# A scan and expert-routing kernel: GpSimd makes every third drive product, a third state buffer, earlier weight loads and separate gates

## The chip, the cores and the metric

The kernel runs on one core of a Trainium2 chip. The metric is the device time of one execution in microseconds (us).

The engines, as the profile names them, are PE (TensorE, matrix products; PEld its weight loads), DVE (VectorE), ACT (ScalarE), POOL (GpSimd) and SP (SyncE, which here only issues DMAs). Each works through its own queue of instructions in order and waits on semaphores for the others. SBUF is the on-chip memory, PSUM the memory in which PE accumulates.

## The reference

Four images of 64x64x3 become 256 tokens each (three levels of patches in Hilbert order, fused by one linear layer) and 128 text tokens are put behind them: 4 sequences of L = 384 tokens with C = 192 features, 1536 tokens in all. Then

```
h = concat(tokenizer(x), txt)
h = h + block(layernorm(h))        # a selective state-space block
h = h + moe(layernorm(h))          # 8 experts, top 2 per token

block:  x, z = split(x @ in_proj.T);  u = silu(causal_conv(x))
        dt = softplus(u @ dt_w.T + dt_b);  B = u @ B_w.T;  C = u @ C_w.T
        state[t] = exp(dt*A) * state[t-1] + dt*B*u        # for 16 states s
        y = sum over s of state*C, + D*u;  y = (y*silu(z)) @ out_w.T
        return layernorm(y + residual) * g + b
moe:    top 2 of h @ Wr.T, gates = softmax of the two
        out = sum of gate_k * (gelu(h @ Wi_e.T + bi_e) @ Wo_e.T + bo_e)
```

## The kernel before, in words

**Stages.** The tokenizer gathers patches with indirect DMAs, PE makes the levels and the fused tokens. Each of three chunks of 128 tokens (of all four sequences at once) is normed, projected, convolved and turned into dt, B and C. B and C rows are written to DRAM (`bc_dram`) and read back broadcast over the partitions. Then come the 48 steps of the scan, the routing, and a loop over 31 tiles of 128 slots each, every tile of one expert.

**A step.** Step `at` is chunk n = at // 16 and state s = at % 16. The instructions of one step lie on all engines:

- PE spreads row B into PSUM, `wide(at % 2)`, and adds up, two steps late, the products of state and C (`sum_states(at - 2)`, L1005 and L1007); between these it has filler and pieces of other stages.
- DVE makes the drive product dt*u*B in place in `wide` (L1752) and then scans (L1760): state = decay * state + drive along the tokens, into `states[at % 2]`. It needs that the product of step at-2 has read that buffer (`hc_rdy`).
- ACT makes the decay (L1437, L1438), saves the last state of each chunk (L1443) and carries it into the next chunk (L1455).
- POOL makes the state product hc = state * C (L697). C rows lie in a ring of RING = 3 buffers, hc in two.
- SP issues the C row three steps ahead (`broadcast_c`, L561 and L563: three DMAs), once the product of step at-3 is made.

In 8 of the 48 steps (at % 6 == 5, `by_pool`) POOL makes the drive as well (L686), from a B row that SP has broadcast to SBUF (`broadcast_b`), into `decay[2]`; DVE then only scans, and ACT puts the decay into PSUM.

**What is put between the steps.** For chunks 1 and 2, DVE handles the chunk before: its output (s = 1), residual (7), scores and the new rows of h (8), the top two (9), a shift (10). ACT writes the router rows (s = 12) into the tile of rows `xf`, SP sends them to `x_dram` (L590) at s = 14 of chunks 1 and 2. SP also issues 20 pieces of expert weights (289 KB each, L583), from step 16 on at steps with at % 4 != 3, and three whole experts after the last sum.

**Routing.** DVE makes from the top two of each token a slot number (counting by PE, prefix sums), then the gates (L1953 to L1956), one-hot tables (L1959 to L1969), which PE turns into a token number for each slot (L1129). POOL fetches the rows of the first four tiles (L706) from `x_dram`, whose rows hold x and, in the last columns, the two gates, sent by L593. It goes once `x_sent` counts all of these. PE meanwhile adds the experts' biases (L1143, L1149) and runs filler. Each tile is transposed (L1161), goes through up (L1171, L1179), gelu on ACT and down (L1190), is scaled by its gate on ACT and added into `sum_dram` by POOL (L722). At the end four DMAs copy it to the output (L639).

Filler are matmuls without use (`keep_warm`, L934), whose number at each place stands in the table `WARM`.

## Time and profile before

| | us |
|---|---|
| runs | 427.67, 433.89, 433.04 |
| median | 433.04 |
| the profiled execution | 433.38 |
| its span | 431.6 |
| granted TensorE clock, mean over the span | 0.941 |

The busy time over the whole span:

| engine | busy us | share |
|---|---|---|
| PE | 379.8 | 88% |
| DVE | 276.2 | 64% |
| POOL | 224.0 | 52% |
| ACT | 200.5 | 46% |

The span is what the trace covers, 1.8 us less than the run's own time. The shares are averages over stages that differ much, and a part of PE's time is filler, so the table alone doesn't tell what sets the time. The stages can be told apart by the lines: steps are L1752, L1760, L697 and L1005, from about 77 to 241 us of the span, and the loop over tiles is L1171 to L1190, from 276 us on.

### The profile page before, as it was taken

How to read it: one execution, taken by the hardware profiler on the slowest of the kernel's cores; microseconds unless marked ns; L12 is line 12 of the kernel's file. 1: busy time of each engine (PE TensorE's matmuls, PEld its weight loads, DVE VectorE, ACT ScalarE, POOL GpSimd, SP SyncE). 2: the span in 40 equal slices, each digit the busy share in tenths (PEclk: the TensorE clock that was granted, in tenths of full speed). 3: DMA queues.
4: the chain of work that ended last, by engine and by line, in shares of the span. 5: the costliest groups of instructions: out<-in, count | busy, mean ns of one | idle time of the engine just before them, and what ended most of it. 6: DMA issues, size and time to landing. Idle time of an engine off the chain costs nothing.

```text
span 431.6 us, 6906 instructions
## 1 busy us (share of the span) xinstructions
PE 379.8 (88%) x2285; PEld 286.8 (66%) x2285; DVE 276.2 (64%) x511; ACT 200.5 (46%) x516; POOL 224.0 (52%) x166
## 2 busy tenths in 40 slices
PE   5799989979996995779968898999999999999970
PEld 4465756646564662445634486799999999999970
DVE  4605456999899998997999596643444534434400
ACT  1347447674853546734547023144444354354440
POOL 6877730564636772756637200345565554655531
PEclk9969899999989996998979997799999999999995
DMA  6401103446574875497857544433333233232224
GB/s 168 78 6 11 7 3 70 122 120 137 116 147 122 232 243 165 158 270 210 294 167 189 150 209 74 113 83 59 49 46 61 43 49 56 44 52 48 39 28 118
DMA packets 37351, 46.98 MB, mean 109 GB/s; under 512 B 9485, under 2 KB 25950, under 8 KB 36750
## 3 DMA queue, kind: packets, MB, share of 16 engines
q1 hardware_dynamic: 29998, 38.94, 32.1%
q0 software_dynamic: 7328, 7.74, 12.2%
q8 instruction: 12, 0.20, 0.2%
q14 instruction: 13, 0.11, 0.1%
HBM read 40.65 MB, written 7.19 MB: 111 GB/s over the span
## 4 chain that ended last, share of the span: by engine, by line
PE 60%; DVE 17%; ACT 6%; DMA 5%; POOL 5%; issue 3%; SPq 1%; POOLq 0%; DVEq 0%; ACTq 0%
PE ps L1190 15%; PE ps L1171 10%; PE ps L1179 6%; DVE w_all L1760 5%; PE ps L1005 4%; DMA w_all<-bc_dram 3%; PE ps L1053 3%; PE ps L934 3%; POOL w_all L647 3%; POOL w_all L697 2%; DVE ps L1752 2%; PE ps L1007 2%; PE ps L1161 2%; DVE stats L1586 1%; DVE h_tok L1807 1%
## 5 line engine op out<-in xcount | busy, mean ns | idle before, releaser
L697 POOL TENSOR_TENSOR w_all<-w_all 128x768 f32<-128x768 f32 x47 | 78.9, 1682 | 82.4 <-DVE w_all L1760 36.6
L722 POOL DMA_INDIRECT sum_dram<-u_cm,tok_row x31 | 50.9, 1641 | 60.5 <-ACT u_cm L1551 53.8
L1005 PE MATMUL ps<-w_all,cst 128*128 128x512 f32 x96 | 55.4, 661 | 22.9 <-POOL w_all L697 22.3
L1760 DVE TENSOR_TENSOR_SCAN w_all<-decay,ps 128x780 f32<-128x780 f32 x40 | 71.1, 1779 | 2.0 <-POOL w_all L697 0.7
L706 POOL DMA_INDIRECT dt_cm<-x_dram,tok_in x31 | 30.8, 993 | 41.0 <-DVE texi L1989 29.0
L647 POOL DMA_INDIRECT w_all<-in_pix,gidx x42 | 44.1, 1051 | 14.9 <-issue 12.5
L1536 ACT ACTIVATE u_cm<-ps,x_cm 128x128 f32<-128x128 f32 x96 | 26.5, 376 | 39.8 <-PE ps L1179 39.8
L934 PE MATMUL ps<-cst 128*128 128x256 f32 x132 | 36.5, 433 | 5.5 <-DMA cst<-in_cst 4.9
L1005 PEld LDWEIGHTS ps<-w_all,cst 128*128 128x128 f32 x96 | 16.5, 198 | 35.4 <-POOL w_all L697 30.4
L1752 DVE TENSOR_TENSOR ps<-dtu_cm,ps 128x768 f32<-128x768 f32 x40 | 38.0, 949 | 2.7 <-ACT ps L1455 2.5
L1536 ACT ACTIVATE z_cm<-ps,y_cm 128x128 f32<-128x128 f32 x90 | 24.8, 375 | 27.5 <-PE ps L1179 27.5
L934 PEld LDWEIGHTS ps<-cst 128*128 128x128 f32 x132 | 28.0, 219 | 12.6 <-DMA cst<-in_cst 4.9
L2001 DVE COPY x_cm<-w_all 128x1154 f32 x16 | 12.2, 762 | 37.1 <-PE ps L1190 37.1
L1007 PEld LDWEIGHTS ps<-w_all,cst 128*128 128x128 f32 x96 | 19.2, 200 | 24.9 <-issue 24.9
L1190 PE MATMUL ps<-x_cm,u_cm 128*128 128x192 f32 x192 | 35.5, 333 | 0.0
L1053 PE MATMUL ps<-cst 128*128 128x256 f32 x122 | 33.6, 401 | 0.0
L1190 PE MATMUL ps<-y_cm,z_cm 128*128 128x192 f32 x180 | 33.4, 334 | 0.0
L2001 DVE COPY y_cm<-w_all 128x1154 f32 x15 | 11.4, 762 | 33.0 <-PE ps L1190 33.0
L1437 ACT ACTIVATE decay<-dt_cm,a_neg 128x512 f32<-128x512 f32 x40 | 28.4, 711 | 8.2 <-DVE dt_cm L1709 8.1
L1190 PEld LDWEIGHTS ps<-x_cm,u_cm 128*128 128x128 f32 x192 | 31.0, 189 | 1.8
L1190 PEld LDWEIGHTS ps<-y_cm,z_cm 128*128 128x128 f32 x180 | 29.0, 189 | 1.8
L1007 PE MATMUL ps<-w_all,cst 128*128 128x256 f32 x96 | 30.1, 396 | 0.0
(268 smaller groups left out, 706.8 us busy)
## 6 DMA issues: line engine op xcount, KB each, us to landing
w_all<-bc_dram SPq DMA_DIRECT2D x48, 256.0 KB, 3.6
w_all<-bc_dram SPq DMA_DIRECT2D x96, 64.0 KB, 3.8
w_all<-in_w_all SPq DMA_DIRECT2D x20, 289.0 KB, 4.5
w_all<-in_w_all SPq DMA_DIRECT2D x3, 1156.0 KB, 8.9
b_wide_sb<-bc_dram SPq DMA_DIRECT2D x8, 256.0 KB, 3.9
x_dram<-x_cm SPq DMA_DIRECT2D x3, 384.0 KB, 4.6
sum_dram<-h_tok SPq DMA_DIRECT2D x3, 384.0 KB, 4.3
out<-sum_dram SPq DMA_DIRECT2D x4, 288.0 KB, 3.7
```

What stands on the lines that cost most here:

```text
L647: pool.indirect_dma_start(dst, None, d[table], bass.IndirectOffsetOnAxis(ap=gidx[:, col:col + 1].bitcast(U32), axis=0)).then_inc(signal, 16)
L697: nc.gpsimd.tensor_tensor(segments(hcs[at % 2]), inner(states[at % 2]), segments(c_sb[at % RING]), ALU.mult).then_inc(hc_rdy, 1)
L722: pool.indirect_dma_start(sum_dram, bass.IndirectOffsetOnAxis(ap=tok_row[:, i:i + 1].bitcast(U32), axis=0), y_out[:, i % 2, :], None, comp ...
L934: nc.tensor.matmul(ps[:, bank, 0:256], ident, cst[:, 0:256], start=True, stop=True)
L1005: nc.tensor.matmul(sums[:, 0:4 * P], ident, hcs[at % 2][:, 0:4 * P], start=False, stop=at % S == S - 1, skip_group_check=True)
L1007: nc.tensor.matmul(sums[:, 4 * P:6 * P], ident, hcs[at % 2][:, 4 * P:6 * P], start=False, stop=at % S == S - 1, skip_group_check=True).the ...
L1053: nc.tensor.matmul(ps[:, bank, 256:512], ident, cst[:, 0:256], start=False, stop=True, skip_group_check=True)
L1171: nc.tensor.matmul(ps[:, 2 + 2 * p + f // 3, P * (f % 3):P * (f % 3) + P], w[:, W_UA + P * f:W_UA + P * f + P], xe[:, p, 0:P], start=(f % ...
L1190: mm = nc.tensor.matmul(ps[:, 6 + p, 0:C], hid[p][:, P * f:P * f + P], w_now[p][:, W_DN + C * f:W_DN + C * f + C], start=(f == 0), stop=(f ...
L1536: ins = nc.scalar.activation(hid[p][:, P * f:P * f + P], ps[:, 2 + 2 * p + f // 3, P * (f % 3):P * (f % 3) + P], ACT.Gelu, bias=w_now[p][: ...
L1752: v.tensor_tensor(inner(wide(p)), chunk(dtu3, n), inner(wide(p)), ALU.mult).then_inc(driven, 1)
L1760: v.tensor_tensor_scan(states[p], fade, drive, 0.0, ALU.mult, ALU.add).then_inc(scanned, 1)
```

## The change

- **Drives on POOL.** `by_pool` is true for every third step from 5 on (5, 8, ..., 47): 15 instead of 8 drives. B rows for them are issued three steps ahead into the one buffer `b_wide_sb`.
- **Third state buffer.** The scan of step `at` writes `states[at % 3]` and needs the product of step at-3 instead of at-2.
- **Weight pieces.** 7 of the 20 pieces are issued right behind the first stored B and C rows, 5 more at the odd steps 7 to 15, the last 8 at every third step from 16 on. For this the tokenizer's temporary tiles, which lie in the weights' memory, are put in another order.
- **Rows and gates apart.** Rows go both to `x_first` and to `x_dram` (two DMAs each), for chunk 0 at step 34 and for chunk 1 after the loop. Gates get a tile and a table of their own (`gate_x`, `gate_dram`). The first four fetches read `x_first` and need only the rows; four fetches of gates follow.
- **Order between the steps.** DVE makes the top two in front of the new h, and the shift a step later; ACT's deviation and router rows move a step later too.
- **Start.** PE's products with the router weights move behind the coarse rows, the first rows of the residual behind the fused tokens; filler is set anew.
- **Routing.** Tables are laid out [k, expert, token], so that operations read in order; the gates' arithmetic moves behind the one-hot tables; the low one-hots are made in four parts; the last product, sum and output of the scan go in halves; the last bias rows move from ahead of the first tile to behind its up projection.
- **Output.** Two of the four final DMAs are issued by ACT.

The core of the diff:

```diff
-        states = [scan_buffer(WIDE) for _ in range(2)]
+        states = [scan_buffer(WIDE) for _ in range(2)] + [third_state[:, :]]
...
-        WARM = {"input weights": 10, "coarse levels": 2, "fine patches": 2, "patches": 7, "normed rows": 7, "convolution": 2,
-                "first step": 10, "last rows": 11, "slots": 20, "bias rows": 1, "first tile": 4}
+        WARM = {"input weights": 10, "coarse levels": 2, "fine patches": 2, "patches": 7, "normed rows": 4, "convolution": 2,
+                "first step": 10, "last rows": 11, "slots": 18, "bias rows": 1, "first tile": 3}
...
-            return at % 6 == 5
+            return at > RING and at % RING == RING - 1
 
         def pool_drives(at):
-            return (at + 1) // 6
+            return max(0, (at + 1) // RING - 1)
 
...
-                if at >= 6:
-                    sp.wait_ge(pool_driven, pool_drives(at - 6))
+                if at >= 2 * RING:
+                    sp.wait_ge(pool_driven, pool_drives(at - RING))
...
+            def rows_of(dst, j, columns):
+                return dst.rearrange("(b j p) c -> j p b c", b=NB, j=NJ)[j, :, :, columns]
 
             def send_rows(j):
                 sp.wait_ge(xf_rdy, j + 1)
-                sp.dma_start(x_rows(j, 0, C), xf[:, NB * j:NB * j + NB, 0:C]).then_inc(x_sent, 16)
+                for dst, signal in ((x_first, x_sent), (x_dram, rows_sent)):
+                    sp.dma_start(rows_of(dst, j, slice(0, C)), xf[:, NB * j:NB * j + NB, 0:C]).then_inc(signal, 16)
+                    sp.dma_start(rows_of(dst, j, slice(C, CW)), xf[:, NB * j:NB * j + NB, P:C]).then_inc(signal, 16)
 
             def send_gates(j):
-                sp.dma_start(x_rows(j, C, XW), xf[:, NB * j:NB * j + NB, P:XF]).then_inc(x_sent, 16)
+                for dst, columns in ((gate_dram, slice(0, TOPK)), (x_dram, slice(CW, XW))):
+                    sp.dma_start(rows_of(dst, j, columns), gate_x[:, NB * j:NB * j + NB, :]).then_inc(gates_sent, 16)
 
             loads = [(e, p) for e in (*range(E - LATE), E - 1) for p in range(PIECES)]
 
             store_bc(0)
+            sp.wait_ge(coarse_ps, 4)
+            sp.wait_ge(rearr, 2)
+            for piece in loads[0:7]:
+                load_expert(*piece, PIECES)
+            loaded = 7
             store_bc(1)
...
-            router_weights()
+            keep_warm(WARM["coarse levels"], 4)
             coarse_levels()
+            pe.wait_ge(ld_mix, 16 * N_MIX)
             pe.wait_ge(x_out, 2)
             dt_low(0)
             dt_high_and_bc(0)
             coarse_rows()
             keep_warm(WARM["fine patches"], 0)
-            first_rows()
...
-                if by_pool(at - RING) and at - RING + 6 < STEPS:
-                    broadcast_b(at - RING + 6)
-                if at > S and at % S == 14:
-                    send_rows(at // S - 1)
+                if by_pool(at) and at + RING < STEPS:
+                    broadcast_b(at + RING)
+                if at == 2 * S + 2:
+                    send_rows(0)
+                if at == 7:
+                    sp.wait_ge(fused_ps, 2)
                 if at == S:
                     sp.wait_ge(xt_ready, 6)
                     sp.wait_ge(dtu_rdy, 3)
+                    sp.wait_ge(mixed_ps, 1)
                 if at == 2 * S + 7:
                     sp.wait_ge(summed, 2 * S + 1)
                     sp.dma_start(u_cm[:, 0:N_TAB // 2], d["cst"][:, N_CST:N_CST + N_TAB // 2]).then_inc(ld_tab, 16)
-                if at >= S and at % 4 != 3 and loaded < len(loads):
+                if (7 <= at < S and at % 2 == 1 or at >= S and at % 3 == 1) and loaded < len(loads):
                     load_expert(*loads[loaded], PIECES)
                     loaded += 1
             assert loaded == len(loads)
...
-                if by_pool(at + RING):
+                if by_pool(at + RING) and at + RING < STEPS:
...
+            def fetch(i, src, columns, signal):
+                pool.indirect_dma_start(x_in[:, i % NX, columns], None, src, bass.IndirectOffsetOnAxis(
+                    ap=tok_in[:, i:i + 1].bitcast(U32), axis=0)).then_inc(signal, 16)
...
+                fetch(i, x_first, slice(0, CW), xin_l[i])
+            pool.wait_ge(gates_sent, 16 * 2 * NJ)
+            for i in range(NX):
+                fetch(i, gate_dram, slice(CW, XW), gate_l[i])
+            pool.wait_ge(rows_sent, 16 * 2 * NJ)
...
+            def last_sum():
+
+                pe.wait_ge(last_hc, 1)
+                nc.tensor.matmul(sums[:, 0:4 * P], ident, hcs[(STEPS - 1) % 2][:, 0:4 * P], start=False, stop=True,
+                                 skip_group_check=True).then_inc(last_low, 1)
+                pe.wait_ge(last_hc, 2)
+                nc.tensor.matmul(sums[:, 4 * P:6 * P], ident, hcs[(STEPS - 1) % 2][:, 4 * P:6 * P], start=False, stop=True,
+                                 skip_group_check=True).then_inc(summed, 1)
 
...
-                if at >= 2:
-                    dve.wait_ge(hc_rdy, at - 1)
-                    if at - 2 < STEPS - S:
-                        dve.wait_ge(carry_saved, at - 1)
-                v.tensor_tensor_scan(states[p], fade, drive, 0.0, ALU.mult, ALU.add).then_inc(scanned, 1)
+                if at >= 3:
+                    dve.wait_ge(hc_rdy, at - 2)
+                    if at - 3 < STEPS - S:
+                        dve.wait_ge(carry_saved, at - 2)
+                v.tensor_tensor_scan(states[at % 3], fade, drive, 0.0, ALU.mult, ALU.add).then_inc(scanned, 1)
...
+                for q in (slice(0, NB), slice(NB, 6)):
+                    v.tensor_tensor(segments(hcs[(STEPS - 1) % 2])[:, q], inner(states[(STEPS - 1) % 3])[:, q],
+                                    segments(c_sb[(STEPS - 1) % RING])[:, q], ALU.mult).then_inc(last_hc, 1)
...
-                        if n == 1:
-                            dve.wait_ge(hb_rdy, NJ)
                         inverse()
                         unscaled_scores(n - 1)
                         router_scores(n - 1)
-                        new_h(n - 1)
-                    elif s == 9:
                         largest(n - 1)
                         its_experts(n - 1)
-                    elif s == 10:
+                    elif s == 9:
+                        if n == 1:
+                            dve.wait_ge(hb_rdy, NJ)
+                        new_h(n - 1)
+                    elif s == 11:
                         row_shift(n - 1)
                     elif at == STEPS - 1:
...
-            v.memset(gate_e8, 0.0).then_inc(dve_set, 1)
...
+            for part in (2, 3, 0, 1):
+                few = slice(NT // 2 * part, NT // 2 * part + NT // 2)
                 at_r += 1
-                assert at_r == ROUTE_LO[1 - k], at_r
-                v.tensor_tensor(at_lo[:, :, half], slot_lo[:, half].rearrange("p (o t) -> p o t", o=1)
...
+                if not is_at_least(i, NX):
+                    dve.wait_ge(gate_l[q], 16)
...
+            act.wait_ge(y_sent, 16 * MT)
+            for b in range(2, NB):
+                act.dma_start(out[b], sum_dram[L * b:L * b + L, :]).then_inc(out_st, 16)
```

On POOL, around step 7 of the scan, before. L697 is the product of state and C, L686 the drive; `w_all` is the memory in which states and products lie.

```order
L697 TENSOR_TENSOR w_all<-w_all 128x768 [waits summed,c_ready2,scanned]
L697 TENSOR_TENSOR w_all<-w_all 128x768 [waits summed,c_ready0,scanned]
L697 TENSOR_TENSOR w_all<-w_all 128x768 [waits c_ready1,summed,conv_step,scanned]
L697 TENSOR_TENSOR w_all<-w_all 128x768 [waits summed,c_ready2,scanned]
L686 TENSOR_TENSOR decay<-dtu_cm,b_wide_sb 128x6x128 [waits scanned,b_ready,dtu_ready]
L697 TENSOR_TENSOR w_all<-w_all 128x768 [waits summed,c_ready0,scanned]
```

The same place after the change, where these are L718 and L707:

```order
L707 TENSOR_TENSOR decay<-dtu_cm,b_wide_sb 128x6x128 [waits scanned,b_ready,dtu_ready]
L718 TENSOR_TENSOR w_all<-w_all 128x768 [waits summed,c_ready0,scanned]
L718 TENSOR_TENSOR w_all<-w_all 128x768 [waits c_ready1,summed,conv_step,scanned]
L718 TENSOR_TENSOR w_all<-third_state,w_all 128x768 [waits summed,c_ready2,scanned]
L707 TENSOR_TENSOR decay<-dtu_cm,b_wide_sb 128x6x128 [waits scanned,b_ready,dtu_ready]
L718 TENSOR_TENSOR w_all<-w_all 128x768 [waits summed,c_ready0,scanned]
L718 TENSOR_TENSOR w_all<-w_all 128x768 [waits summed,c_ready1,scanned]
```

A drive now stands behind every third product, before behind every sixth.

On SP, where chunk 0's router rows are sent (L590), before; L561 and L563 are broadcasts of a C row, L583 a weight piece:

```order
L563 DMA w_all<-bc_dram 64x256 x2
L583 DMA w_all<-in_w_all 128x578
L561 DMA w_all<-bc_dram 128x512 [waits hc_rdy]
L563 DMA w_all<-bc_dram 64x256 x2
L590 DMA x_dram<-x_cm 128x4x192 [waits xf_rdy]
L583 DMA w_all<-in_w_all 128x578
L561 DMA w_all<-bc_dram 128x512 [waits hc_rdy]
L563 DMA w_all<-bc_dram 64x256 x2
```

After, with L571 and L573 the broadcasts (`b_wide_sb` is the B row for POOL), L601 and L602 the rows, L593 a piece:

```order
L571 DMA w_all<-bc_dram 128x512 [waits hc_rdy]
L573 DMA w_all<-bc_dram 64x256 x2
L571 DMA w_all<-bc_dram 128x512 [waits hc_rdy]
L573 DMA w_all<-bc_dram 64x256 x2
L601 DMA x_first<-x_cm 128x4x192 [waits xf_rdy]
L602 DMA x_first<-x_cm 128x4x64
L601 DMA x_dram<-x_cm 128x4x192
L602 DMA x_dram<-x_cm 128x4x64
L593 DMA w_all<-in_w_all 128x578
```

The rows moved from between the C rows of steps 30 and 31 to behind that of step 34, four DMAs instead of one, and a B row stands between the C rows of every third step.

On DVE, in the routing, from the slot numbers (L1949, L1950) over the gates to the one-hot tables, before:

```order
L1949 TENSOR_SCALAR b_parts<-decay 128x24 [waits route]
L1950 TENSOR_TENSOR b_parts<-decay,b_parts 128x24 [waits route]
L1953 TENSOR_SCALAR gtmp<-gtmp 128x12 [waits gate_e,route]
L1954 RECIPROCAL x_cm<-gtmp 128x12 [waits route]
L1955 TENSOR_TENSOR gate<-gtmp,x_cm 128x12 [waits route]
L1956 TENSOR_TENSOR x_cm<-gate,x_cm 128x12 [waits route]
L1959 TENSOR_TENSOR pick<-b_parts,u_cm 128x744 [waits ld_tab,route]
L1961 TENSOR_SCALAR pick<-pick,cst 128x744 [waits route]
L1962 TENSOR_TENSOR pick<-pick,u_cm 128x744
L1969 TENSOR_TENSOR pick<-b_parts,u_cm 128x128x12 x2
```

After; slot numbers are L2002 and L2003, one-hot tables L2005 to L2015, gates L2018 to L2026:

```order
L2002 TENSOR_SCALAR b_parts<-decay 128x24 [waits route]
L2003 TENSOR_TENSOR b_parts<-decay,b_parts 128x24 [waits route]
L2005 TENSOR_TENSOR pick<-b_parts,u_cm 128x744 [waits ld_tab,route]
L2007 TENSOR_SCALAR pick<-pick,cst 128x744 [waits route]
L2008 TENSOR_TENSOR pick<-pick,u_cm 128x744
L2015 TENSOR_TENSOR pick<-b_parts,u_cm 128x128x6 x4
L2018 TENSOR_TENSOR gtmp<-top_v 128x12
L2019 TENSOR_TENSOR gtmp<-gtmp,rstd 128x12 [waits route]
L2023 TENSOR_SCALAR gtmp<-gtmp 128x12 [waits gate_e,route]
L2024 RECIPROCAL gate_x<-gtmp 128x12 [waits route]
```

The gates' arithmetic went from ahead of the one-hot tables to behind them, and the last table is made in four instructions instead of two.

## Rows read from the trace of the kernel before

**Rows 1.** Busy time by windows: start:end, us, PE, PEld, DVE, ACT, POOL, clock, DMA, GB/s.

```profile
77.30:240.90 163.60, 138.23 (x598) 83.33 (x597) 152.88 (x211) 93.77 (x220) 98.00 (x58) 0.94 0.64 178
240.90:276.20 35.30, 31.91 (x155) 24.42 (x153) 23.97 (x90) 5.91 (x12) 4.01 (x4) 0.85 0.45 139
276.20:418.20 142.00, 142.00 (x1176) 133.55 (x1176) 61.24 (x123) 63.98 (x216) 75.41 (x57) 1.00 0.33 54
```

**Rows 2.** Timeline, DVE, last steps: start, duration, engine, line, operation; [idle <-releaser] where it waited.

```profile
233.61 1.78 DVE L1760 TENSOR_TENSOR_SCAN w_all<-decay,ps 128x780 f32<-128x780 f32 x1
...
236.28 1.78 DVE L1760 TENSOR_TENSOR_SCAN w_all<-decay,ps 128x780 f32<-128x780 f32 x1
238.02 1.78 DVE L1760 TENSOR_TENSOR_SCAN w_all<-ps,decay 128x780 f32<-128x780 f32 x1
```

**Rows 3.** Timeline, DVE, waits within the scan stage.

```profile
115.28 1.78 DVE L1760 TENSOR_TENSOR_SCAN w_all<-ps,decay 128x780 f32<-128x780 f32 x1 [1.77 <-POOL w_all L697]
...
164.09 0.18 DVE L1602 RECIPROCAL rstd<-std 128x4 f32<-128x4 f32 x1 [0.93 <-ACT std L1306]
...
182.36 0.96 DVE L1752 TENSOR_TENSOR ps<-dtu_cm,ps 128x768 f32<-128x768 f32 x1 [0.24 <-ACT ps L1455]
...
201.01 0.96 DVE L1752 TENSOR_TENSOR ps<-dtu_cm,ps 128x768 f32<-128x768 f32 x1 [2.24 <-ACT ps L1455]
```

**Rows 4.** Chain of waits around 180 us: start, duration, what it led through.

```profile
180.01 1.76 ACT x_cm L1462 x4
181.78 0.44 SPq L590
...
185.96 4.94 DMA w_all<-bc_dram
```

**Rows 5.** The page's DMA issues: C rows, KB each, median us to landing.

```profile
w_all<-bc_dram SPq DMA_DIRECT2D x48, 256.0 KB, 3.6
```

**Rows 6.** Timeline, POOL, a drive (L686) and the product behind it.

```profile
176.66 1.82 POOL L686 TENSOR_TENSOR decay<-dtu_cm,b_wide_sb 128x768 f32<-128x768 f32 x1
178.42 1.69 POOL L697 TENSOR_TENSOR w_all<-w_all 128x768 f32<-128x768 f32 x1
```

**Rows 7.** Timeline, SP's queue: a B row, a piece, a C row, a piece.

```profile
186.84 0.58 SPq L561 DMA_DIRECT2D b_wide_sb<-bc_dram  x1
...
188.60 0.59 SPq L583 DMA_DIRECT2D w_all<-in_w_all  x1
189.23 0.43 SPq L561 DMA_DIRECT2D w_all<-bc_dram  x1
...
190.84 0.58 SPq L583 DMA_DIRECT2D w_all<-in_w_all  x1
```

**Rows 8.** Timeline, DVE, the last step's product of state and C.

```profile
240.90 0.96 DVE L1836 TENSOR_TENSOR w_all<-w_all 128x768 f32<-128x768 f32 x1 [1.09 <-DMA w_all<-bc_dram]
```

**Rows 9.** Timeline, DVE, routing: first gate operation, first one-hot table, token numbers.

```profile
259.38 0.17 DVE L1953 TENSOR_SCALAR gtmp<-gtmp 128x12 f32<-128x12 f32 x1
...
260.29 0.55 DVE L1959 TENSOR_TENSOR pick<-b_parts,u_cm 128x744 bf16<-128x744 bf16 x1
...
266.88 0.18 DVE L1980 TENSOR_SCALAR tok_in<-decay 128x31 int32<-128x31 f32 x1
```

**Rows 10.** Timeline, routing: gate columns (SP), first fetch (POOL), last bias rows, first up (PE).

```profile
260.67 1.92 SPq L593 DMA_DIRECT2D x_dram<-x_cm  x3
...
268.85 0.97 POOL L706 DMA_INDIRECT dt_cm<-x_dram,tok_in  x1 [29.03 <-DVE texi L1989]
...
270.07 1.95 PE L1149 MATMUL ps<-bo,z_cm 8*128 8x192 f32 x8
...
276.16 1.58 PE L1171 MATMUL ps<-u_cm,x_cm 128*128 128x128 f32 x12 [0.56 <-issue]
```

**Rows 11.** Busy time of PE in the window of the first residual rows.

```profile
39.02:41.54 2.52, 2.52 (x21) 1.00 0.13 5
```

**Rows 12.** Timeline, SP's queue, the four stores of the output.

```profile
424.94 2.46 SPq L639 DMA_DIRECT2D out<-sum_dram  x4
```

264 lines of the change are left out of this document (144 added, 120 removed).

## The prediction

> **What bounds the kernel now.** I read the busy time by windows first [rows 1]. The scan stage, 77.3 to 240.9 us, has VectorE (DVE) busy for 152.88 of 163.60 us. PE (138.23) and GpSimd (POOL, 98.00) have room, and the DMA engines are busy 0.64 of the time. The routing between the scans and the first expert matmul takes 35.30 us, with no engine full except PE, which runs filler. The expert loop is all PE: 142.00 of 142.00 us, clock 1.00. So the scans hang on DVE, the routing on a chain of short operations, and the loop on matmuls that the change leaves alone.
>
> Next come DVE's rows around an ordinary step [rows 2]. Scan to scan is 236.28 − 233.61 = 2.67 us where DVE makes both the drive product and the scan, and 238.02 − 236.28 = 1.74 us where GpSimd has made the product. So a drive that moves to GpSimd gives back 0.93 us of DVE. Then the stalls [rows 3]: 1.77 us on GpSimd's state product at 115.28 (the state buffer), 0.93 on ACT's standard deviation, 0.24 at 182.36 and 2.24 at 201.01 on the carry, both in a drive product.
>
> The chain of waits explains the last of these [rows 4]. ACT's router rows end at 181.78, SP stood waiting for them and only then issues, then come weight loads and the broadcasts queued behind, and a C row that needs 4.94 us to land, at 190.90. GpSimd's product, PE's sum and the carry follow from it. The page has 3.6 us as the median landing of such rows [rows 5].
>
> **What the change costs and gives, scan stage.** Seven more drives (steps 8, 14, 20, 26, 32, 38, 44) leave DVE: 7 × 0.93 = 6.5 us at most.
>
> What GpSimd then needs: a state product takes 1.69 and starts the next no more than that later, a drive 1.82 but the product behind it starts 1.76 after it [rows 6]. Three steps need 3 × 1.66 + 1.76 = 6.7 us (3 × 1.69 + 1.82 = 6.9 without the overlap), DVE 2 × 2.67 + 1.74 = 7.1 us. GpSimd stays under DVE by 0.2 to 0.4 us per three steps. This holds only while nothing else is inserted on GpSimd.
>
> What SP needs: a B row holds its queue from 186.84 to 188.60 = 1.76, a weight piece to 189.23 = 0.63, a C row to 190.84 = 1.61 [rows 7]. Three steps after the change issue three C rows, one B row and, from step 16 to 37, one piece: 4.83 + 1.76 + 0.63 = 7.2 us. That is just above DVE's 7.1. Before, six steps issued six C rows, one B row and four or five pieces, 6 × 1.61 + 1.76 + 4.5 × 0.63 = 14.3 us against DVE's 5 × 2.67 + 1.74 = 15.1. SP so comes level with the bound during the 22 steps that carry pieces, costing 0.1 us for three steps (7 times) and a little at the B rows, 1 us in all. A second loop of the same kind: a C row's buffer comes free at its product, its issue is 1.6, landing 3.6, product 1.7: 6.9 us for three steps, but 8.2 if landings stay at the 4.94 of [rows 4].
>
> There is also the hand-over by carry: the product that ended at 180.11 [rows 6] let the drive go at 182.36 [rows 3], 2.25 us later, through PE's sum and ACT. Where GpSimd inserts a drive (1.82), the next state product, PE's sum and, queued behind it, the spread of the next B row are that much later. The third state buffer takes the scan itself off this loop but not PE's order. I take 0.1 us for each of the 15 steps, 1.5 in all, with 0 and 4 as ends (the far one is 0.24 of [rows 3] for each of 15 steps).
>
> Gains beside it: SP no longer meets the router rows at step 30 (they are sent at 34 and after the loop). Of 2.24 us at 201.01 I take 1.3 as removed. The 0.93 at 164.09 goes, since ACT's decay for step 26 no longer stands ahead of the deviation. The 1.77 at 115.28 is one stall at a point where table load and decay are close behind, I take 0.3. The last product (0.96 at 240.90 [rows 8]) is made in halves, so that PE sums the first under the second: 0.5. DVE waited 1.09 there for the last C row, whose queue is less late after the change: I take 0.6 of it.
>
> Sum: 6.5 − 1 − 1.5 + 1.3 + 0.9 + 0.3 + 1.1 = 7.6, less 1.4 for steps 18 to 22, where GpSimd has a drive (20) beside its residual add and the sum of 18 comes late for the drive of 21 (a drive's 1.82 [rows 6] less the 0.4 of room). That leaves 6.2; I use **6** us, with 3 and 8 as ends.
>
> **Weights from the first stage.** Seven pieces start while the tokenizer runs, where no broadcast is in the queue; I cost them at nothing. What hides them is SP's idle time before the first stored B and C rows. If the queue or the landing delayed these rows, the first steps would start later by up to 7 × 0.63 = 4.4 us. I keep 0, since SP waits for stores of the first chunk anyway.
>
> **Start.** PE's router-weight matmuls move off the way of the coarse levels; the first rows of the residual (2.52 us on PE [rows 11]) move behind the fused tokens, ahead of the second norm transposes, with two filler matmuls of their own, while the filler there falls from 7 to 4. What the earlier place gives back is the same 2.52, and the filler nets to one matmul fewer. I take 0, with ±1.
>
> **Routing tail.** Four gate operations on 128x12 leave the path ahead of the one-hot tables: 260.29 − 259.38 = 0.91 us [rows 9], so 0.23 each. Two more such and the memset leave with them, 0.7; one operation less stands before the token numbers, 0.2. The layouts that DVE now reads and writes in order (three operations) and the low one-hots in quarters instead of halves, which let PE start sooner, I take at three such operations together, 0.7, with 0 and 1.4 as ends. Token numbers, ready at 266.88 + 0.18 = 267.06, come 2.5 us earlier, at 264.5.
>
> The first fetch went at 268.85 and waited not for them but for the gate columns, whose three DMAs were issued from 260.67 to 262.59: 6.26 us of landing [rows 10]. The fetches now read a table with the row columns alone. These were sent just ahead of 260.67; with 3.6 us of landing [rows 5] they are there at 264.3, with 4.94 [rows 4] at 265.6. The fetch goes at about 264.8, **4.0** us earlier. Before, PE ran filler until the first tile, whose up projection at 276.16 had only 0.56 us of issue before it [rows 10]; so PE's own order was as late as the fetched rows. After the change that order is shorter by the 2.5 us of the token numbers, by filler (20 to 18, 4 to 3) and by the last bias rows, 1.95 us [rows 10], and ends near 270; rows fetched at 264.8 are there by 272 at the latest (276.16 − 4.0). These bias rows now lie between the first and the second up projection. I take the first up projection from 276.16 to 270, 6.2 us, less 1.95: **4.3** us for the first down projection and all tiles behind it, with 2 (the fetch's 4.0 less 1.95) and 5.5 (the bias rows mostly under the wait for the second fetch) as ends.
>
> The gates' own path is longer: ready between 260.67 (as now) and 264.5 (the token numbers stand behind them), say 261.5; six DMAs at 0.64 (1.92 for three) take 3.8, landing 6.26: 271.6, or 274.6 at worst. The gate fetches, an issue of 0.97 each [rows 10] and a landing like the others, bring tile 0's gates at about 275.5. Its output is scaled behind its down projection, with the second tile's up ahead of it on PE: one and a half tile periods (142.00 / 31 = 4.58 us [rows 1]) behind the first up, about 277. So some 2 us of slack hide them, and none at worst. If that cover is gone, tile 0's output is late, then its PSUM bank, and the loop stalls.
>
> **Stores of the output.** Four issues in a row took 2.46 us [rows 12]; two queues of two take 1.2. I take **1.0**. The Trainium skill (DMA: Bandwidth & Descriptors, Issuing engines are not separate DMA queues) says that issuing on several engines saves only the sequencers' time, as the same 16 DMA engines carry it. The trace agrees that issue is a visible part; by the rule nothing beyond the 1.2 can come.
>
> **Sum.** The profiled span was 431.6 us in a run of 433.38, so 1.8 lie around it. 431.6 − 6 − 0 − 4.3 − 1.0 = 420.3, plus 1.8 = **422 us**. Against the median of the three runs, 433.04, this is 2.5% faster; that profile lies 0.3 above the median.
>
> **Rivals.** (A) *SP or GpSimd becomes the bound of the steps.* For: SP's 7.2 and GpSimd's 6.7 to 6.9 against DVE's 7.1, and landings at 4.94 make the C loop 8.2. Against: most landings are nearer 3.6, and the pieces are thinner per step than before. If the period becomes 7.55 for the 15 triples, as much as half of the 15.1 of before, the 6.5 are gone and only 2 of the stage's 6 remain: 426 us.
>
> (B) *The routing gain is lost.* Gate rows or weights land later than the slack (they share the DMA engines with three late experts' weights). For: the gates' slack is only 2 us. Then only 0 to 1 of the 4.3 remain: 425 to 426 us.
>
> (C) *Slower: GpSimd slows DVE or SP falls behind for good.* If landings stay at 4.94 and the triple takes 8.2, 15 × (8.2 − 7.55) = 9.8 us are lost, against tail and other gains of 7: 436 us; from a triple of 8.0 on it outweighs the tail's gain. Against: [rows 7] were taken under the heaviest loads and DVE still ran at its pitch. The Trainium skill (GPSIMD Engine Reference, Specifications) says that GpSimd shares VectorE's SBUF interfaces and contends with DVE instructions that read two SBUF operands. The scans and drives here have one operand in PSUM, and the scan at 236.28 took 1.78 like the others. By the rule only work such as conversions of new rows would slow, a few tenths.
>
> (D) *No effect in the steps*: DVE's idle moves to waits on PE and ACT, whose sum and carry stay at one per step. Gain 2 there: 426 us, like (A).
>
> **Chances and range.** Forecast, 418 to 424.4: 0.50. A or D, 424.4 to 429: 0.25. B, 0.13. C, 0.06. Better than 418, everything at its upper end (8 + 5.5 + 1.2 + 1 gives 417.7): 0.06. The range **416 to 430** leaves out C, the worst of A and B together, and half of the best case: 0.15 to 0.2. A difference over 2% can be told from no change here, so the edges lie at 424.4 and 441.7. Faster 0.56, same 0.41 (C's 436 is within), slower 0.03, for C with a triple beyond 8.6.
>
> **What would show it.** Right: between pool-driven scans 7.0 to 7.2 us per three steps; first fetch 10 us earlier than 268.85, the first up projection near 264 instead of 276.16; 142 us of loop unchanged. Wrong: DVE waits with GpSimd or DMA named at most steps, SP issuing without a break through the steps (A), a wait for the gate columns ahead of the loop (B), scans above 1.78 (C), or gates and fetches with a late first output.

## The result and the profile after

The changed kernel is slower: 440.26 us (median of 4; 436.78 to 440.83, a fifth execution on record took 443.22) against 431.85 for the kernel before beside it (427.67 to 433.89), a ratio of 1.021 (95%: 1.011 to 1.030); the interval doesn't settle whether that is more than 2%. Its profiled execution took 436.78 (span 434.8), that of before 433.38 (span 431.6), so the two traces hold 3.2 of some 8 us. Some executions of a kernel run at a lower clock and take some per cent longer: the ratios below leave them out, so they need not be the quotient of the two medians beside them, and the traces of rows_late and one_set are of such executions.

Busy time by windows of after, as [rows 1]: the steps, the routing, the loop. Columns: start:end, us, PE, PEld, DVE, ACT, POOL, clock, DMA, GB/s.

```profile
78.38:241.70 163.32, 134.62 (x570) 81.01 (x569) 149.46 (x203) 93.69 (x220) 110.05 (x65) 0.95 0.65 187
241.70:277.00 35.30, 32.33 (x140) 22.41 (x139) 23.29 (x92) 6.02 (x12) 4.90 (x6) 0.85 0.65 160
277.00:421.90 144.90, 144.62 (x1184) 135.60 (x1184) 63.30 (x126) 64.29 (x217) 80.90 (x60) 0.99 0.32 53
```

DVE's work in the steps fell by 3.4 us, GpSimd's rose by 12, and the window is as long as it was. The routing, up to the first up projection, is as long as well. The last window, from there on, is 2.9 longer; the milestones show that nearly all of this lies between the first up and the first down projection (5.2 us before, 7.8 after). By milestones (us; before, after):

| stretch | before | after | forecast |
|---|---|---|---|
| start to first scan | 78.25 | 79.33 | 0 ± 1 |
| first to last scan | 159.77 | 160.66 | 4.9 less |
| last scan to first down | 43.31 | 44.84 | 5.4 less |
| first down to last scatter | 140.15 | 140.34 | 0 |
| last scatter to end | 10.12 | 9.63 | 1.0 less |

(The forecast's 1.1 us for the last product, which it counts in the scan stage, lie behind the last scan and stand in the third line here.)

**Where nothing intervenes, the steps do what was forecast.** DVE's timeline of after (start, duration, operation), three steps apart:

```profile
179.95 1.75 DVE L1809 TENSOR_TENSOR_SCAN third_state<-ps,decay 128x780 f32<-128x780 f32 x1
...
186.96 1.76 DVE L1809 TENSOR_TENSOR_SCAN third_state<-ps,decay 128x780 f32<-128x780 f32 x1
```

That is 7.01 us, against the 7.1 of the forecast. The page's group of scans also stands unslowed (last columns: busy, mean ns, idle before):

```profile
L1809 DVE TENSOR_TENSOR_SCAN w_all<-decay,ps 128x780 f32<-128x780 f32 x32 | 56.9, 1779 | 1.1
```

**The new stall.** SP's queue of after at step 34, where the forecast saw a gain because the router rows no longer stand at step 30:

```profile
190.84 0.59 SPq L601 DMA_DIRECT2D x_first<-x_cm  x1
191.46 0.51 SPq L602 DMA_DIRECT2D x_first<-x_cm  x1
192.01 0.90 SPq L601 DMA_DIRECT2D x_dram<-x_cm  x1
192.96 0.89 SPq L602 DMA_DIRECT2D x_dram<-x_cm  x1
193.90 1.20 SPq L593 DMA_DIRECT2D w_all<-in_w_all  x1
...
196.78 0.59 SPq L571 DMA_DIRECT2D b_wide_sb<-bc_dram  x1
```

Four row DMAs hold the queue for 3.06 us. In the chain of waits the B row behind them then needs 5.85 us to land:

```profile
198.22 5.85 DMA b_wide_sb<-bc_dram
```

and GpSimd and DVE pay (timelines of both, GpSimd's row first):

```profile
202.39 1.67 POOL L718 TENSOR_TENSOR w_all<-third_state,w_all 128x768 f32<-128x768 f32 x1 [4.88 <-DMA b_wide_sb<-bc_dram]
...
206.44 1.78 DVE L1809 TENSOR_TENSOR_SCAN third_state<-ps,decay 128x780 f32<-128x780 f32 x1 [3.42 <-POOL decay L707]
...
210.65 0.96 DVE L1801 TENSOR_TENSOR ps<-dtu_cm,ps 128x768 f32<-128x768 f32 x1 [2.42 <-ACT ps L1500]
```

The 2.24 us of [rows 3] at 201.01 went and 5.84 came.

**The wait of the state buffer changed its cause.** At step 11 GpSimd's product no longer holds the scan ([rows 3], 1.77 at 115.28), but ACT's decay does (DVE's timeline of after), for longer:

```profile
117.02 1.78 DVE L1809 TENSOR_TENSOR_SCAN third_state<-ps,decay 128x780 f32<-128x780 f32 x1 [2.08 <-ACT ps L1483]
```

**The routing.** Timeline of after, from the slot matmuls to the first down projection, to be held against [rows 10]:

```profile
261.10 6.82 PE L1167 MATMUL ps<-pick 128*128 128x186 bf16 x24 [0.19 <-DVE pick L2015]
268.73 0.98 POOL L727 DMA_INDIRECT dt_cm<-x_first,tok_in  x1 [26.89 <-DVE decay L2037]
275.84 0.69 PE L1206 MATMUL ps<-cst,dt_cm 128*128 128x128 f32 x2 [1.95 <-DMA dt_cm<-x_first,tok_in]
277.04 2.93 PE L1216 MATMUL ps<-u_cm,x_cm 128*128 128x128 f32 x12 [0.52 <-DVE u_cm L2063]
284.83 2.23 PE L1237 MATMUL ps<-x_cm,u_cm 128*128 128x192 f32 x12
```

In the chain of waits the fetch's landing is

```profile
268.73 7.06 DMA dt_cm<-x_first,tok_in
```

Against the last scan, the slot matmuls start 3.5 us earlier than before (21.1, not 24.6). Then the matmuls that turn one-hots into token numbers take 6.82 instead of 3.60, since the change feeds them the columns of `what` twice ([2, 3, m] in place of [3, m]). The fetch goes 2.1 earlier (28.74 behind the last scan, 30.83 before), lands in 7.06, PE waits 1.95 for it and multiplies the first tile at half clock (granted clock 0.5), 2.93 instead of the 1.58 of [rows 10].

### The profile page after: what moved, and what is told of

Its sections match the earlier page's. It is cut to its first block, busy times and chain, and to the rows that moved or that the text cites. A ratio compares the mean times of both kernels' runs of the same rounds, so it can differ in the third digit from the quotient of the medians.

```text
span 434.8 us, 6889 instructions
## 1 busy us (share of the span) xinstructions
PE 380.2 (87%) x2253; PEld 285.8 (66%) x2253; DVE 274.2 (63%) x508; ACT 200.9 (46%) x516; POOL 242.4 (56%) x177
## 4 chain that ended last, share of the span: by engine, by line
PE 48%; DVE 20%; POOL 12%; DMA 6%; issue 6%; SPq 3%; ACT 2%; POOLq 0%; DVEq 0%; ACTq 0%
PE ps L1237 15%; PE ps L1216 10%; PE ps L1224 6%; POOL w_all L668 6%; DVE w_all L1809 5%; POOL w_all L718 4%; PE ps L1031 3%; DVE ps L1801 3%; DMA b_wide_sb<-bc_dram 2%; DVE y_cm L1754 2%; SPq L573 2%; PE ps L1206 2%; DMA dt_cm<-x_first,tok_in 2%; PE ps L1167 2%; PE ps L961 2%
## 5 line engine op out<-in xcount | busy, mean ns | idle before, releaser
L718 POOL TENSOR_TENSOR w_all<-w_all 128x768 f32<-128x768 f32 x32 | 53.7, 1680 | 55.8 <-DVE w_all L1809 27.2
L747 POOL DMA_INDIRECT sum_dram<-u_cm,tok_row x31 | 52.2, 1684 | 54.5 <-ACT u_cm L1596 26.4
L1809 DVE TENSOR_TENSOR_SCAN w_all<-decay,ps 128x780 f32<-128x780 f32 x32 | 56.9, 1779 | 1.1
L1581 ACT ACTIVATE z_cm<-ps,y_cm 128x128 f32<-128x128 f32 x90 | 24.9, 375 | 28.7 <-PE ps L1224 28.7
L1801 DVE TENSOR_TENSOR ps<-dtu_cm,ps 128x768 f32<-128x768 f32 x33 | 31.3, 949 | 5.2 <-ACT ps L1500 5.1
L727 POOL DMA_INDIRECT dt_cm<-x_dram,tok_in x27 | 27.8, 1030 | 11.5 <-issue 7.9
L718 POOL TENSOR_TENSOR w_all<-third_state,w_all 128x768 f32<-128x768 f32 x15 | 25.2, 1679 | 15.7 <-DMA b_wide_sb<-bc_dram 5.4
L1809 DVE TENSOR_TENSOR_SCAN third_state<-ps,decay 128x780 f32<-128x780 f32 x15 | 26.5, 1766 | 5.5 <-POOL decay L707 3.4
```

Source lines behind the costliest of these rows:

```text
L718: nc.gpsimd.tensor_tensor(segments(hcs[at % 2]), inner(states[at % 3]), segments(c_sb[at % RING]), ALU.mult).then_inc(hc_rdy, 1)
L727: pool.indirect_dma_start(x_in[:, i % NX, columns], None, src, bass.IndirectOffsetOnAxis(ap=tok_in[:, i:i + 1].bitcast(U32), axis=0)).then ...
L747: pool.indirect_dma_start(sum_dram, bass.IndirectOffsetOnAxis(ap=tok_row[:, i:i + 1].bitcast(U32), axis=0), y_out[:, i % 2, :], None, comp ...
L1581: ins = nc.scalar.activation(hid[p][:, P * f:P * f + P], ps[:, 2 + 2 * p + f // 3, P * (f % 3):P * (f % 3) + P], ACT.Gelu, bias=w_now[p][: ...
L1801: v.tensor_tensor(inner(wide(p)), chunk(dtu3, n), inner(wide(p)), ALU.mult).then_inc(driven, 1)
L1809: v.tensor_tensor_scan(states[at % 3], fade, drive, 0.0, ALU.mult, ALU.add).then_inc(scanned, 1)
```

## The experiments

Theory **S**: the steps' gain is lost at the four row DMAs of step 34, and a little at the hand-over by carry. Rival **P**: the drives overload GpSimd or SP everywhere. Theory **R**: the routing's gain is lost in the doubled columns, and in a fetch whose rows land late because the gates' DMAs stand before it. Rival **C**: it is the clock.

On some chips used here the tokenizer is slower by some 38 us, whatever the kernel (the patches are fetched as early, the products on them come later): the kernel before takes 471 to 473 us there and 432 to 435 on the others. Ratios are always to the kernel before on the same chip. "Steps" is from the first to the last scan, "up" and "down" are the first such projections, from the last scan; "loop" is from the first down to the last scatter.

**a_again.** No edit: the changed kernel once more, as the base of comparison.

> The changed kernel unchanged, to see on this chip where its runs of 440 us stand against its profiled run of 436.8. If the loss lies in fixed places (1.1 us at the start, 0.9 in the steps, 1.5 in the routing), the ratio is about 1.01 and the profile shows the same three places. If it is a matter of how the DMAs and the clock fall out, the profile shows another place that is several us longer.

482.38 (477.0 to 487.4) against 470.75 us. Steps 161.5, fetch 28.7, up 37.5, down 48.2. Here the half clock reaches past the first tile (windows, columns as above):

```profile
308.00:322.00 14.00, 11.09 (x54) 8.06 (x54) 6.20 (x14) 0.62 (x3) 7.71 (x8) 0.50 0.41 38
```

The down projection comes 3.4 us later than in the profile of after. So the changed kernel has executions with a longer half clock, which can be the part of the 8 us that the profile of after does not hold; the runs at 440 were not traced.

**rows_late.** The rows of chunk 0 are sent after the loop.

```diff
-                if at == 2 * S + 2:
-                    send_rows(0)
...
+            send_rows(0)
             send_rows(1)
```

> The changed kernel, with the rows of chunk 0 sent after the loop instead of at step 34. Theory (SP's queue): the four row DMAs and the piece behind them held the queue from 190.84 to 195.10 us, so that the B row of step 38 came at 204.07 and DVE stood 3.42 + 2.42 us; without them the two waits go, the last scan comes 4 to 6 us earlier, and the run is 3 to 5 us shorter (about 435 us). Rival (GpSimd has no room): the wait at step 38 stays or comes back at the next drive, gain under 1 us.

471.22 against 470.75, 0.996 (0.991 to 1.002). Steps 155.7, 5.8 less than a_again; the waits at steps 38 and 39 are gone but for 0.72. Theory S holds in place and size. What is left are the 2.08 at step 11 and five waits on the carry, 3.6 us in all, the longest at step 21 (DVE's timeline):

```profile
196.04 0.96 DVE L1800 TENSOR_TENSOR ps<-dtu_cm,ps 128x768 f32<-128x768 f32 x1 [1.55 <-ACT ps L1499]
```

and what leads to it, on PE and ACT: PE waits for GpSimd's product, sums, and only then spreads B, on which ACT's carry waits.

```profile
193.85 1.13 PE L1030 MATMUL ps<-w_all,cst 128*128 128x512 f32 x2 [1.64 <-POOL w_all L717]
194.81 0.59 PE L1032 MATMUL ps<-w_all,cst 128*128 128x256 f32 x2
195.24 0.27 PE L1011 MATMUL ps<-b_parts,pick 128*128 128x256 bf16 x1
...
195.83 0.18 ACT L1499 ACTIVATE ps<-carry 128x6 f32<-128x6 f32 x1 [2.77 <-PE ps L1014]
```

**two_rows.** Only the two DMAs into `x_first` stay at step 34; the two into `x_dram` go after the loop.

```diff
                 for dst, signal in ((x_first, x_sent), (x_dram, rows_sent)):
+                    if dst is x_dram and j == 0:
+                        continue
```

> The changed kernel, with only two of the four row DMAs at step 34 (those into x_first; the two into x_dram go behind the loop). It tells the queue's time from the DMAs' load: the four held SP's queue 3.1 us, and the B row of step 38 then needed 5.85 us to land instead of 3.6. Theory (queue time and load both): the waits at steps 38 and 39 fall from 3.42 + 2.42 us to 1 to 3 in all, the steps take 157 to 158.5 us (after 160.7, rows_late 155.7). If the queue alone were the cause, the first two DMAs' 1.2 us would remain and the steps take about 157; if the load of the x_dram copies alone were, 155.7.

433.67 (10 runs) against 434.76, 0.999 (0.994 to 1.004). Steps 156.6: of the 160.7 of after, the second copy costs 4.1 us, the first 0.5 to 1.1 (rows_late and the other kernels with late rows and this order: 155.5 to 156.0). That lies between what the queue's time alone (157) and the copies' load alone (155.7) would leave, so the two aren't separated. One wait is left there:

```profile
210.49 0.96 DVE L1805 TENSOR_TENSOR ps<-dtu_cm,ps 128x768 f32<-128x768 f32 x1 [1.84 <-ACT ps L1504]
```

**steps_only.** The kernel before with nothing but drives at every third step, three state buffers and B rows three steps ahead.

```diff
-            return at % 6 == 5
+            return at > RING and at % RING == RING - 1
...
-        states = [scan_buffer(WIDE) for _ in range(2)]
+        states = [scan_buffer(WIDE) for _ in range(2)] + [third_state[:, :]]
```

> The kernel before with three things alone: every third drive product on GpSimd, B rows for them three steps ahead, and a third state buffer. Forecast's theory (seven drives leave DVE): the scan stage gets 4 to 7 us shorter, 426 us. Rival (SP's queue is full: C rows, a B row and two or three pieces per three steps take 4.83 + 1.76 + 1.4 = 8.0 us against DVE's 7.1): the stage gains nothing or loses up to 4 us, DVE waits with GpSimd's drive or the carry named, 431 to 436 us.

473.2 (466.1 to 475.0) against 470.75. Steps 159.60, before 159.77: no gain. Two waits on the carry take it. Ahead of the first, SP issues broadcasts and pieces without a break from 173.4 to 185.9, a C row goes out at 180.66 and lands only in 4.78 us, and the carry comes late (chain of waits, DVE's timeline):

```profile
181.15 4.78 DMA w_all<-bc_dram
```

```profile
190.11 0.96 DVE L1753 TENSOR_TENSOR ps<-dtu_cm,ps 128x768 f32<-128x768 f32 x1 [3.53 <-ACT ps L1456]
```

The other, of 2.82 us at 230.84, comes behind two landings of 4.30 and 3.95; in SP's queue chunk 0's router rows (220.77) and a piece stand ahead of the second. So with pieces and router rows where they were before, the drives alone bring nothing: rival P is right for this kernel, through SP and at two places. Which of the two matters more isn't separated.

**six.** rows_late with the drives back at every sixth step, three state buffers kept.

```diff
-            return at > RING and at % RING == RING - 1
+            return at % 6 == 5
```

> rows_late with GpSimd's drives at every sixth step as before, all else as changed (three state buffers, early weights, order of the inserted work). rows_late took 155.7 us from the first to the last scan, the kernel before 159.8. Forecast's theory (each moved drive takes 0.93 us from DVE): the stage takes 155.7 + 6.5 = 162. Rival (in the pool steps the carry behind GpSimd's product gives half of it back, the gain came from the other edits): 156 to 159.

438.51 against 435.41, 1.007 (1.000 to 1.015). Steps 158.7, against 155.7 to 156.0 with every third (rows_late, start_lean, copies_late and copies_filler agree in that): the seven drives give back 2.7 to 3.0 us of the 6.5. The wait on the standard deviation is back, with 0.98 us at 165.48, so that its going belongs to the drives too.

**spread_first.** rows_late, with PE's spread of the next B row put ahead of the sum of step at-2.

```diff
+                if S <= at < STEPS - 1:
+                    spread_b(at + 1)
                 if at >= 2 and (n == 0 or s != 2):
                     sum_states(at - 2)
```

> rows_late, with one order changed on PE: in chunks 1 and 2 the spread of the next step's B row stands ahead of the sum of two steps back, not behind it. rows_late (drives at every third step) took 155.8 us from first to last scan, six 158.7; seven moved drives should give 6.5 and gave 2.9. Theory (hand-over on PE: the sum waits for a state product that stands behind GpSimd's drive, and the spread, the carry and DVE's drive wait behind that sum; waits of 1.55, 0.47, 0.41, 0.48 and 0.72 us in rows_late): these waits go, the stage takes 152 to 153 us. Rival (SP or GpSimd has no room either): the waits come back with GpSimd's drive or a DMA named, 155 or more.

469.27 against 470.9, 0.988 (0.981 to 0.995) on record, while the medians differ by 0.3%. Steps 153.0, 2.7 less than rows_late and 2.4 less than gates_hold, gates_split and start_filler on this chip (155.5 each); the waits on the carry are gone but for 0.2 us. The hand-over is now shown: it cost 2.4 to 2.7 us, the wait at step 21 included.

**one_set.** The changed kernel, its slot matmuls reading the columns once.

```diff
-  mm = nc.tensor.matmul(ps[:, 7, 0:6 * MT] ..., at_lo[:, :, t], what ... .to_broadcast([P, 2, w, MT]), ...
+  mm = nc.tensor.matmul(ps[:, 7, 0:w * MT] ..., at_lo[:, :, t], what[:, 0:w, :, t], ...
```

> The changed kernel, with the slot matmuls' 186 or 124 columns made 93 or 62 again (the second copy was not read). Theory: the columns cost 6.82 - 3.60 = 3.2 us on the way to the first fetch; without them the token numbers come 3 us earlier and the loop starts 2 to 3 us earlier, 437 us. Rival (the strided weights and four waits make it long, not the columns): the 24 matmuls still take over 6 us and nothing moves. Second rival: the time is won but the TensorE clock stays at half speed for longer, and the loop starts at the same time.

482.17 (469.9 to 483.7) against 470.75, too scattered for a ratio; steps 162.2. The matmuls take 3.60, the token numbers and the fetch come 3.1 us earlier (25.6), as theory R said. But up gains 1.0 only, as the fetch now meets the gates' DMAs head on (chain of waits):

```profile
310.66 9.61 DMA dt_cm<-x_first,tok_in
```

**copies_late.** rows_late and one_set; `x_dram` is written only after four fetches have landed, gates go to `gate_dram` alone.

```diff
+            for i in range(NX):
+                sp.wait_ge(xin_l[i], 16)
+            sp.dma_start(x_dram[:, 0:CW], x_first[:, :]).then_inc(rows_sent, 16)
```

> rows_late and one_set together, and the copies of rows and gates into x_dram are issued only when the first four fetches have landed (rows from x_first, gates from their tile). one_set brought the first fetch from 28.7 to 25.6 us behind the last scan, but its row landed at the same time, 10.9 us later instead of 7.1. Theory (the small descriptors of the row and gate copies stand in the DMA rings ahead of the fetch): landing goes back to about 6.3 us, the first up projection comes 3 to 4 us earlier than in one_set (33 instead of 36.5 behind the last scan). Rival (PE's filler and the bias rows hold it): the up projection stays at 36.

433.61 against 435.41, 0.988 (0.977 to 0.999). Three gate DMAs are still ahead of the fetch, and its landing is 8.13 us. Up 35.0, down 43.2, but DVE then waits 1.00 for the first gate row, the fifth fetch waits for its table, and the loop takes 144.0.

**copies_filler.** The same with 8 instead of 3 filler matmuls ahead of the first tile.

```diff
-  "first tile": 3
+  "first tile": 8
```

> copies_late with 8 instead of 3 filler matmuls ahead of the first tile (before: 4, of two widths' time each). The first up projection took 2.93 us in the changed kernel at a granted clock of 0.5, 1.58 at 1.0 before. Theory: a PE that does not idle ahead of the tile brings the clock back, the first up takes 1.6 and the down projection comes 1 us earlier. Rival: the filler itself takes the place of the wait and the tile starts as much later as it gains.

435.11 against 435.41, 1.00 (0.991 to 1.009). The first up takes 1.60 (full clock; 2.29 in copies_late) and down comes at 40.9. Rival C holds for these 2 us. The number of filler isn't what decides: gates_split has eight as well, but PE waits 1.60 for the fetch and the first up takes 2.90; combined has three, doesn't wait and takes 1.60. Of eighteen traces, the eleven in which PE waited 1.6 us or more for the fetch all show a slowed first up (2.29 to 2.93), and of the seven without this wait only combined_hold does (2.93). The loop then takes 147.7: DVE waits 3.86 for the first gate row, and the fifth fetch waits for its table (GpSimd's timeline), so that everything is given back.

```profile
284.74 1.28 POOL L730 DMA_INDIRECT dt_cm<-x_dram,tok_in  x1 [8.79 <-DMA x_dram<-gate_x]
```

**gates_hold.** rows_late, one_set, 8 filler; the six gate DMAs wait until the first fetch has landed.

```diff
             sp.wait_ge(route, ROUTE_GATES)
+            sp.wait_ge(xin_l[0], 16)
```

> rows_late, one_set and 8 filler matmuls ahead of the first tile, and the six DMAs of the gates held until the first fetched row has landed. In after, rows_late, one_set, copies_late and copies_filler the first fetch landed at the moment at which the gates' DMAs did, whenever it had been issued (7.1 to 9.7 us before). Theory (the fetch stands in the rings behind the gates' 8-byte descriptors, so that taking the gates off the fetch's semaphore gains nothing): the fetch lands within 5 us, first up at 31 to 32 us behind the last scan; the gates then come too late and the first output waits. Rival (a fetch of 128 rows takes 7 to 8 us whatever is in the rings): first up at 34 or later.

471.75 against 470.9, 1.004 (0.999 to 1.008). The chain of waits shows both sides of the bargain:

```profile
297.10 3.45 DMA dt_cm<-x_first,tok_in
...
303.32 10.65 DMA x_dram<-gate_x
```

The fetch lands in 3.45 us when nothing of the gates is in flight; the gates then take 10.65, and the loop 146.5. Up stands at 35.6, held by the eight filler.

**gates_split.** rows_late, one_set, 8 filler; the gates' `x_dram` part is issued behind the token numbers.

```diff
+            sp.wait_ge(route, ROUTE_FLAGS)
+            for j in range(NJ):
+                sp.dma_start(rows_of(x_dram, j, slice(CW, XW)), gate_x[...]).then_inc(gates_copied, 16)
```

> rows_late, one_set, 8 filler matmuls, and of the gates' six DMAs the three into x_dram issued only behind the token numbers. copies_filler had its first down projection at 40.9 us behind the last scan (before 43.3) but lost 7.5 in the loop, since the copies for the fifth fetch came late. Theory: first down at 41, loop 140.3 us as before, 2 us shorter than rows_late's and before's routing; ratio about 0.985. Rival: the x_dram copies still land too late for the fifth fetch and the loop takes 142 or more.

467.68 against 470.9, 0.987 (0.982 to 0.993) on record, while the medians differ by 0.7%. The landing did not shorten: 10.72, up 37.3. By copies_late (8.13) the three DMAs into `gate_dram`, still ahead, are enough to delay the fetch; that the other three now fall on it is the likely rest. Of the 4.2 us by which its span is below that of gates_hold, 1.7 lie ahead of the last scan.

**start_lean.** rows_late without the filler between the fused tokens and the second norm's transposes.

```diff
-  "normed rows": 4
+  "normed rows": 0
...
-                keep_warm(2, 0)
                 token_rows(0, 5, 64)
```

> rows_late, and without the 4 filler matmuls ahead of the second norm transposes and the 2 within the first residual rows. In the changed kernel the fused tokens are done at 47.2 us (52.3 before), but PE then runs first rows and filler at a granted clock of 0.5 to 0.6 until 56.5, while the normed tokens it waits for were ready at 50.9. Theory (PE's own order holds the transposes): the time from the last fused-token matmul to the first norm transpose falls from 9.3 to about 5 us and the steps start 4 us earlier. Rival (the half clock is the cause and idle time keeps it there): what the filler leaves is lost behind it, the steps start at most 1 us earlier.

433.22 against 435.41, 0.997 (0.990 to 1.004). The transposes come 5.2 us behind the start of the fused tokens (10.4 in rows_late, also at 0.56), as the theory said, and the first scan 30.4 instead of 33.5 behind it. So 3.1 of 5.2 us stay; the rest is lost because the half clock, which lasts some 13 us behind the start of the fused tokens here as there, now falls on the products behind the transposes. Against the order of before, with 27.5 at full clock, 2.9 us are still missing.

**start_filler.** rows_late with 4 instead of 1 filler behind the patches' transposes.

```diff
-            keep_warm(1, 7)
+            keep_warm(4, 7)
             fine_level(0)
```

> rows_late with 4 instead of 1 filler matmul between the patch transposes and the fine level. Where the patches came early (after, six) PE waited 1.3 us there for DVE's router weights, and the clock was 0.5 to 0.6 from 47.2 us on; from the last fused-token matmul to the first scan it took 32.1 us. Where they came late (copies_late) there was no such wait, the clock was 1.0 and it took 27.3. Theory (the wait brings the clock down): with the gap filled the clock stays at 1.0 and this stretch takes 27 to 28 us. Rival (the clock falls there whatever PE does): 32 us as before where the patches come early.

470.45 against 470.9. The clock behind the fused tokens was 1.00, but so it was without that filler in spread_first on this chip. Inconclusive by itself; but six kernels whose clock fell there (rows_late among them) had PE wait no more than 0.25 us at this place, so the 1.3 us wait isn't needed for the fall.

**combined.** rows_late, spread_first, one_set, and all gate DMAs behind the token numbers, those into `gate_dram` first.

```diff
-            sp.wait_ge(route, ROUTE_GATES)
+            sp.wait_ge(route, ROUTE_FLAGS + 3)
```

> The four causes taken out together: chunk 0's rows after the loop, the spread ahead of the sum, one set of slot columns, and the gates' DMAs issued only behind the token numbers, so that they stand behind the first fetch (those of gate_dram first, those of x_dram behind them). Theory (these are the causes): steps 153 us (before 159.8), fetch landing in 3.5 to 5 us, first down projection at 36 to 38 us behind the last scan (before 43.3, changed 44.8), loop 140.3; in all 10 to 13 us shorter than before, ratio about 0.975. Rival (the gates now come too late for the first tiles): loop 143 to 146 us, ratio 0.985. Rival 2 (a half clock at the first tile takes it back): first down at 40 or later.

464.97 against 472.53, 0.987 (0.980 to 0.994). Steps 152.5. The first fetch is now ahead of the gates, up comes at 30.9, at full clock. The third fetch meets them instead (chain of waits, PE's timeline):

```profile
294.78 9.94 DMA dt_cm<-x_first,tok_in
...
304.76 0.69 PE L1210 MATMUL ps<-cst,dt_cm 128*128 128x128 f32 x2 [1.79 <-DMA dt_cm<-x_first,tok_in]
```

Down 42.9, loop 140.8. Behind the fused tokens the clock was 0.60, and it took 32.0 us from there to the first scan.

**combined_start.** The same with the start of before (router weights, first rows, filler).

```diff
-            keep_warm(WARM["coarse levels"], 4)
+            router_weights()
             coarse_levels()
...
             fused_tokens(0)
-            first_rows()
```

> combined, with the order of the start as before (router weights ahead of the coarse levels, first rows ahead of the interpolation, 7 filler matmuls). In seven of twelve profiles with the changed start the TensorE clock fell to 0.5 or 0.6 behind the fused tokens and the way from there to the first scan took 32 instead of 27 us; in both profiles with the order of before it stayed at 1.0 and took 26. Theory (the changed start brings the clock down in a part of the runs): with the old order the clock stays at 1.0 there, and the runs scatter less, median 0 to 3 us below combined's. Rival (it falls by chance in either order): the same scatter, and the start 0 to 2 us later where the clock stays up.

461.97 (7 runs) against 472.53, 0.978 (0.973 to 0.983). From the fused tokens to the first scan 27.3 us at a clock of 1.00.

**combined_hold.** The same with the gates' DMAs held until the first fetch has landed.

```diff
-            sp.wait_ge(route, ROUTE_FLAGS + 3)
+            sp.wait_ge(route, ROUTE_GATES)
+            sp.wait_ge(xin_l[0], 16)
```

> combined_start, with the gates' DMAs held until the first fetched row has landed instead of until the token numbers. In combined and combined_start the first fetch landed 4 to 5 us behind its issue and the first up came at 30.9 and 31.8 us behind the last scan (before 38.1), but the third fetch took 9.9 us, landed with the gates' DMAs, and the first down projection waited for it (42.9 and 41.6, before 43.3). Theory (whatever fetch stands behind the gates' small descriptors waits for them): the third fetch lands within 5 us, the first down comes at 37 to 38; the gates' own path is 2 us later and the loop takes 140.3 to 143: ratio 0.965 to 0.975. Rival (the gates are then too late): the loop takes 145 or more and the ratio stays at 0.978.

423.97 against 434.76, **0.976 (0.968 to 0.983)**, faster than the kernel before. Its spans against those of before: first scan 74.78 (3.5 earlier), steps 152.55 (7.2 less), down 40.95 (2.4 less), loop 142.89 (2.7 more). How much of the 3.5 us at the start belongs to the change isn't shown: the fused tokens, which come ahead of it, began anywhere from 45.2 to 48.3 us in the seven changed kernels of the faster chips and at 50.8 in the one trace of before. The loop's loss is visible on DVE, whose first gate operation waits for the gate row, with the copies for later tiles queued behind it, and PE behind these:

```profile
265.97 0.94 POOL L729 DMA_INDIRECT dt_cm<-gate_dram,tok_in  x1 [8.13 <-DMA gate_dram<-gate_x]
...
269.71 0.22 DVE L2070 SCALAR_TENSOR_TENSOR gate_q<-dt_cm,decay 128x1 f32<-128x1 f32 x1 [2.89 <-DMA dt_cm<-gate_dram,tok_in]
...
273.13 1.60 PE L1217 MATMUL ps<-u_cm,x_cm 128*128 128x128 f32 x12 [2.41 <-DVE u_cm L2064]
```

**The routing and the loop of all of them together** (us from the last scan; the last column is down plus loop):

| kernel | fetch | landing | up | down | loop | to last scatter |
|---|---|---|---|---|---|---|
| before | 30.8 | | 38.1 | 43.3 | 140.2 | 183.5 |
| after | 28.7 | 7.1 | 37.1 | 44.8 | 140.3 | 185.2 |
| a_again | 28.7 | 7.5 | 37.5 | 48.2 | 140.2 | 188.5 |
| one_set | 25.6 | 9.6 | 36.5 | 44.8 | 141.2 | 186.0 |
| gates_split | 25.6 | 10.7 | 37.3 | 45.3 | 141.5 | 186.8 |
| copies_late | 25.6 | 8.1 | 35.0 | 43.2 | 144.0 | 187.2 |
| copies_filler | 25.6 | | 34.5 | 40.9 | 147.7 | 188.6 |
| gates_hold | 25.6 | 3.5 | 35.6 | 42.0 | 146.5 | 188.5 |
| combined | 25.6 | 9.9 (third) | 30.9 | 42.9 | 140.8 | 183.7 |
| combined_start | 25.6 | | 31.8 | 41.6 | 144.2 | 185.8 |
| combined_hold | 25.6 | | 32.1 | 41.0 | 142.9 | 183.8 |

No layout reaches the last scatter sooner than the kernel before. The first down came up to 2.4 us earlier, and all of it came back in the loop, where the traces show waits for gate rows or for the table that the fifth fetch reads.

## Why the prediction was wrong

The forecast was 422 us within 416 to 430; the profiled execution took 436.8, the median 440.3. Two steps of it failed, each by more than 5 us: the router rows in the scan stage, and the routing (doubled columns and the landing of the first fetch). Of the 8 us between the two medians, about 5 lie outside the two traces, and what they are stays open (a longer half clock at the loop's start, as in a_again, is possible). By its own steps:

- **"So a drive that moves to GpSimd gives back 0.93 us of DVE"**: the pitch was right (7.01 us for three steps). Of 6.5 us, 2.7 to 3.0 came (six against the kernels with every third); the hand-over took most of the rest.
- **The hand-over by carry, "1.5 in all, with 0 and 4 as ends"**, and the 1.4 "for steps 18 to 22": right in mechanism and size. Together they are 2.9; spread_first gave 2.4 to 2.7 back by taking PE's spread from behind the sum. The 1.4 was forecast to the place: DVE waits 1.55 at step 21 in rows_late, 1.30 in after.
- **"SP no longer meets the router rows at step 30 ... I take 1.3 as removed"**: this is the step that failed in the scan stage. It counted what left step 30 and not what came to step 34: four DMAs, 3.06 us of queue in front of a B row due three steps later, which then needed 5.85 us to land. The stall at step 36 did go (2.24), but 5 to 6 us were lost at steps 38 and 39 (after and a_again against rows_late), 4.1 of them to the second copy (two_rows). With the rows out of the way the steps took 155.5 to 156.0, 3.8 to 4.3 less than before, near the forecast's 4.9. The diff shows four DMAs for one, and the prediction's own SP budget (7.2 us against 7.1) left no place for them.
- **Standard deviation, state buffer, order between the steps**: all that is not drives gave 1.1 us in the steps with the rows out of the way (before 159.8, six 158.7), where the forecast had 0.9 + 0.3 + 1.3 = 2.5. The deviation's stall stayed in six (0.98) and went only with the drives. The state buffer took GpSimd's product off the scan of step 11, but ACT's decay held it, 1.58 in six and 2.08 in after, for 1.77 before. And the later shift, priced at nothing, cost 2.1 us (last section).
- **Weights from the first stage, 0**: no trace shows a cost, but no run took this edit out alone.
- **Start, "0, with ±1"**: +1.1 in the profile, but out of two larger terms. The fused tokens came 5.0 us earlier (45.8 instead of 50.8; combined_hold, with the old order, 47.5, so that much of this is not the order). From there to the first scan it took 33.5 instead of 27.5. Ahead of the fused tokens PE waited 1.29 for DVE's router weights; behind them its first rows and filler ran at a low clock:

```profile
43.98 1.04 PE L848 MATMUL ps<-w_all 48*64 48x512 f32 x2 [1.29 <-DVE w_rt L1664]
45.79 1.57 PE L868 MATMUL ps<-w_all 65*128 65x192 f32 x8
...
56.52 1.06 PE L880 MATMUL ps<-cst,xn 128*128 128x128 f32 x4
```

with, in the windows (columns as above),

```profile
47.20:56.50 9.30, 9.30 (x33) 8.05 (x33) 3.00 (x13) 1.76 (x8) 7.00 (x8) 0.54 0.13 20
```

  In the order of before the clock stood at 1.00 behind the fused tokens in all four traces (before, steps_only, combined_start, combined_hold), and the first scan came 27.3 to 27.5 us behind the start of these. In the changed order it was 0.50 to 0.62 in nine of fourteen traces, 0.8 in one, with 30 to 35 us in these ten, and 1.00 in four, with 28.7. So the step that failed here is "the same 2.52" given back: the first rows and their filler stand between the fused tokens and the transposes, which come 6.6 instead of 5.2 to 5.4 us behind even at full clock, and the clock adds 1.7 to 6.6 us in ten of fourteen traces. What decides it stays open. PE had no idle time in this window, so it is not a gap just there.
- **Routing, "4.3 us for the first down projection"**: the second step that failed; it came 1.5 later. The path on DVE was right (slot matmuls 3.5 us earlier, forecast 2.5 + 1.1). Missing was the doubled column operand of the slot matmuls, 3.2 us, an edit that the working never costs. The fetch's landing was assumed as before; it was 7.06, behind the gates' DMAs, where it is 3.45 undisturbed. And the earlier PE order was no gain: PE waited 1.95 for the fetch, and the first tile ran at half clock (2.93 for 1.58).
- **Gates with "some 2 us of slack"**: with the first down at 44.8, they were on time. But the slack ends there: with the gates sent as early as in after, DVE waits 1.00 for the first gate row where the down comes at 43.2 (copies_late) and 3.86 where it comes at 40.9 (copies_filler). Had the rest of the forecast come true, with the down at 43.3 − 5.4 = 37.9, rival B would likely have set in. Its price, "0 to 1 of the 4.3 remain", is even above the table, where the best case (combined) is 0.2 us worse than before.
- **Stores, 1.0**: the end took 0.49 us less in after, but in spread_first, gates_hold and combined_hold, with the same four stores, 10.4 to 10.5 us, no less than the 10.12 of before. The gain, in no trace over 0.6 us, lies below the 1.2 of issue time. The Trainium skill (DMA: Bandwidth & Descriptors, Issuing engines are not separate DMA queues) says that several issuing engines save only the sequencers' time; this agrees.
- **Rivals.** A came nearest in the steps: its SP side in steps_only and at step 34, at places rather than as a period. C, the only slower one, named SP falling behind "for good" and was given 0.06; SP fell behind once, with 5 to 6 us, and that was enough.

Range and chances were too narrow for the same reason as the sum: each rival was priced alone, the edits that add work (second copies, doubled columns) had no term at all, and the range left out C, the only rival above 433.

## What to carry to other kernels

When a queue runs level with the bound, every DMA that a moved step issues needs a price, and the diff should be read once for nothing but operands and DMAs that grew. A transfer that is issued earlier is worth nothing if it lands no earlier: here six DMAs of 3072 pieces of 8 bytes in all stood before it. An order that looks equal on TensorE may run at another clock, so its time is to be read from several traces. Before an earlier start of a loop is counted, look for the next input that the loop needs (here gates and the second table): its time is the floor.

## What the hardware showed

**Some DVE operations wait for GpSimd.** The shift, an operation on 128x4, took as long as the GpSimd product beside it (timelines of DVE and POOL in after), where it took 0.16 us in the kernel before (at 174.73):

```profile
231.37 1.68 DVE L1865 SCALAR_TENSOR_TENSOR shift<-mv,rstd 128x4 f32<-128x4 f32 x1
```

```profile
231.34 1.68 POOL L718 TENSOR_TENSOR w_all<-w_all 128x768 f32<-128x768 f32 x1 [0.99 <-DVE w_all L1809]
```

Likewise 0.77 us at 176.58, where it ends with GpSimd's drive, and the first operation of the convolution, on 128x524, took 1.83 at 101.83, before 0.47 at 100.77. All in all some 3.5 us of after, which the forecast had at "a few tenths". Scans and drive products, with one operand in PSUM, kept their 1779 and 949 ns, and a reciprocal of 128x4 beside a drive its 0.15 (176.39).

For the shift this is not the price of more drives. It takes 0.77 and 1.67 in six too, which has eight drives, and 0.16 in steps_only, which has fifteen (timelines of DVE in six and in steps_only):

```profile
229.18 1.67 DVE L1864 SCALAR_TENSOR_TENSOR shift<-mv,rstd 128x4 f32<-128x4 f32 x1
```

```profile
265.16 0.16 DVE L1817 SCALAR_TENSOR_TENSOR shift<-mv,rstd 128x4 f32<-128x4 f32 x1
```

It came with the shift's later place, which falls beside a product or a drive, while GpSimd was idle in the old one: 2.1 us in every kernel with the changed order of the steps. The convolution's operation is slow in some traces with fifteen drives (steps_only, rows_late) and not in others (a_again, copies_late, 0.49).

The Trainium skill (GPSIMD Engine Reference, Specifications) says that GpSimd shares SBUF interfaces with VectorE, with contention for DVE instructions that have two SBUF inputs or run in a 2-port mode. The shift, with two SBUF tensors, and the spared scans agree; the convolution's operation reads one tensor and a factor per partition, and no row shows its mode. Yet an operation of the top two on 128x8, with two SBUF inputs, kept its 0.16 beside a product (171.38 in before), so what decides isn't settled. Where it happened, the price was the rest of GpSimd's instruction.

**A gathered fetch behind small pieces.** 128 rows landed in 3.45 us with the gates held back, and in 7.1 to 10.7 us behind three or six DMAs with 8 bytes per token; the last of six such DMAs needed 10.65 us itself (gates_hold).
